# High and low part of a product's weights interleaved element by element

## What is computed

```python
x = fwht(x * SU_ug) / SCALE                       # 4096 tokens of 512
x_up = x @ W_up.T * (Wscale_ug[:INTER] * SCALE)    # INTER = 2048
x_gate = x @ W_gate.T * (Wscale_ug[INTER:] * SCALE)
x = silu(x_gate) * x_up
x = fwht(x * SU_dp) / SCALE
x = x @ W_down.T * (Wscale_dp * SCALE)
```

## Time and profile before

| | |
|---|---|
| median of 3 runs | 1592.2 us (1590.52 to 1594.0) |
| the profiled execution, its own time | 1590.71 us |
| its span, first to last instruction | 1588.9 us |
| granted TensorE clock, mean | 0.993 |
| PE busy | 1537.9 us (97%) |
| weight loads (PEld) busy | 1385.6 us (87%) |
| DVE busy | 1040.3 us (65%) |
| ACT busy | 616.2 us (39%) |
| POOL busy | 465.6 us (29%) |

### The profile page before, as it was taken

How to read it: one execution, slowest core, us unless ns; L and a number is a source line. 1 busy time by engine, 2 the same in 40 slices (tenths; PEclk the granted TensorE clock), 3 DMA queues, 4 the chain that set the end, 5 groups by cost and what they waited for, 6 DMA issues and landing times.

```text
span 1588.9 us, 26579 instructions
## 1 busy us (share of the span) xinstructions
PE 1537.9 (97%) x10280; PEld 1385.6 (87%) x10280; DVE 1040.3 (65%) x1771; ACT 616.2 (39%) x1257; POOL 465.6 (29%) x584
## 2 busy tenths in 40 slices
PE   6999999999998799999999999999999999999997
PEld 5987988888887688889999999999999999999996
DVE  6766776677676699875575475566466557557544
ACT  4153244235225555433433343343343333333322
POOL 5365456447337533500030030030040021013001
PEclk9999999999999999999999999999999999999999
DMA  7031122122222497587668677857776867766861
GB/s 270 1 120 60 34 87 93 34 81 100 70 77 84 185 374 275 212 293 278 236 218 297 220 253 246 279 204 257 268 245 220 307 203 258 276 242 212 281 229 63
DMA packets 92060, 307.44 MB, mean 193 GB/s; under 512 B 9888, under 2 KB 10272, under 8 KB 90144
## 3 DMA queue, kind: packets, MB, share of 16 engines
q1 hardware_dynamic: 90928, 301.54, 53.8%
q10 hardware_dynamic: 1008, 4.20, 0.7%
HBM read 255.37 MB, written 50.33 MB: 192 GB/s over the span
## 4 chain that ended last, share of the span: by engine, by line
PE 61%; DVE 5%; ACT 1%; DMA 1%; issue 1%; SPq 0%; POOL 0%; ACTq 0%; POOLq 0%; DVEq 0%
PE ff_bank_b L1840 16%; PE ff_bank_c L1840 10%; PE ff_bank_a L1840 10%; PE ff_acc L105 7%; PE ff_acc L107 7%; PE ff_acc L106 7%; DVE ff_d_lo L1639 2%; DMA gu_scratch<-ff_ring 1%; DVE ff_ring L1629 1%; PE ff_x_ps L1791 1%; ACT at_union L578 1%; PE ff_x_ps L1811 1%; PE ff_x_ps L1799 0%; DVE ff_c L1685 0%; PE ff_x_ps L1800 0%
## 5 line engine op out<-in xcount | busy, mean ns | idle before, releaser
L1840 PE MATMUL ff_bank_b<-ff_x_hi,ff_ring 128*128 128x256 f32 x1536 | 303.5, 280 | 4.5 <-DVE ff_c L1685 4.2
L1840 PEld LDWEIGHTS ff_bank_b<-ff_x_hi,ff_ring 128*128 128x128 f32 x1536 | 248.6, 188 | 6.3 <-issue 4.5
L1840 PE MATMUL ff_bank_b<-ff_x_lo,ff_ring 128*128 128x256 f32 x768 | 214.7, 280 | 0.0
L105 PE MATMUL ff_acc<-ff_d_hi,ff_h_hi 128*128 128x512 f32 x512 | 203.9, 398 | 2.7 <-DVE ff_d_lo L1639 2.7
L1840 PE MATMUL ff_bank_c<-ff_x_hi,ff_ring 128*128 128x256 f32 x1024 | 205.8, 284 | 0.0
L1840 PE MATMUL ff_bank_a<-ff_x_hi,ff_ring 128*128 128x256 f32 x1024 | 203.5, 282 | 0.0
L107 PE MATMUL ff_acc<-ff_d_hi,ff_h_lo 128*128 128x512 f32 x512 | 199.8, 390 | 0.0
L106 PE MATMUL ff_acc<-ff_d_lo,ff_h_hi 128*128 128x512 f32 x512 | 199.4, 389 | 0.0
L1840 PEld LDWEIGHTS ff_bank_c<-ff_x_hi,ff_ring 128*128 128x128 f32 x1024 | 166.2, 189 | 2.2 <-issue 2.0
L1840 PEld LDWEIGHTS ff_bank_a<-ff_x_hi,ff_ring 128*128 128x128 f32 x1024 | 165.3, 188 | 2.7 <-DVE ff_ring L1629 0.2
L1679 DVE TENSOR_TENSOR ff_c<-ff_bank_b,ff_c 128x512 f32<-128x512 f32 x64 | 44.2, 690 | 163.8 <-PE ff_bank_b L1840 163.8
(11 more groups left out here) (306 smaller groups left out, 3523.7 us busy)
## 6 DMA issues: line engine op xcount, KB each, us to landing
ff_ring<-gu_scratch SPq DMA_DIRECT2D x392, 512.0 KB, 4.9
gu_scratch<-ff_ring SPq DMA_DIRECT2D x56, 512.0 KB, 7.6
at_xt<-in_xt SPq DMA_DIRECT2D x4, 2048.0 KB, 8.4
at_xn<-in_x SPq DMA_DIRECT2D x32, 256.0 KB, 3.0
x_scratch<-at_x SPq DMA_DIRECT2D x32, 256.0 KB, 2.0
ff_raw<-in_wgu SPq DMA_DIRECT2D x8, 1024.0 KB, 7.7
at_wd_a<-in_wd SPq DMA_DIRECT2D x8, 512.0 KB, 4.1
mixed_scratch<-at_wd_a SPq DMA_DIRECT2D x8, 512.0 KB, 3.5
```

Source lines behind the costliest of these rows:

```text
L105: pe.matmul(out, lhs_hi, rhs_hi, start=first, stop=False)
L1840: i = pe.matmul(bank[:, m, :], r[:, a, m, c, :], b[:, k, c, :], start=(k < 3 and m == 0 and c == 0 and b is x_hi and a == 0), stop=(m == 1 ...
```

## The change

The tile's shape goes from [part, m, c, column] to [m, c, column, part]: the high and the low part of an element lie side by side, 4 bytes each. The scratch in DRAM has the same shape. So the ACT and the DVE instruction that make the tile write every second element (and DVE reads the high part in that step), and a weight load reads 128 elements with a step of 8 bytes between them, where they were packed at 4. The transfers move the same 4 KB of each partition in one piece. The token tiles of block 0 in slots 5 to 7 keep their place and are packed: the new function `half` gives for them the same views that `both` gave before.

```diff
-        ring = [sb(f"ring{i}", [P, 2, 2, 2, P], F32R) for i in range(RING)]
+        ring = [sb(f"ring{i}", [P, 2, 2, P, 2], F32R) for i in range(RING)]
@@
         def both(slot, part):
-            return ring[slot][:, part, :, :, :].rearrange("p m c n -> p (m c n)")
-
-
-        begin_hi = [xs_hi[:, :], both(5, 0), both(6, 0), both(7, 0)]
-        begin_lo = [xs_lo[:, :], both(5, 1), both(6, 1), both(7, 1)]
+            return ring[slot][:, :, :, :, part].rearrange("p m c n -> p (m c n)")
+
+        def half(slot, part):
+            return ring[slot][:, part, :, :, :].rearrange("p c n a -> p (c n a)")
+
+        begin_hi = [xs_hi[:, :], half(5, 0), half(6, 0), half(7, 0)]
+        begin_lo = [xs_lo[:, :], half(5, 1), half(6, 1), half(7, 1)]
@@
-                            i = pe.matmul(bank[:, m, :], r[:, a, m, c, :], b[:, k, c, :], start=(k < 3 and m == 0 and c == 0 and b is x_hi and a == 0),
+                            i = pe.matmul(bank[:, m, :], r[:, m, c, :, a], b[:, k, c, :], start=(k < 3 and m == 0 and c == 0 and b is x_hi and a == 0),
@@
-    gu_dram = nc.dram_tensor("gu_scratch", [PRODUCTS, P, 2, 2, 2, P], F32, kind="Internal").ap()
+    gu_dram = nc.dram_tensor("gu_scratch", [PRODUCTS, P, 2, 2, P, 2], F32, kind="Internal").ap()
```

## The result

The changed kernel takes 1605.3 us as the median of four runs (1603.3 to 1608.3), the kernel before 1592.1 in the same comparison: 1.0087 times as long, 95% interval 1.0074 to 1.0099. It is slower by some 13 us. The forecast was no change, with 0.26 for slower; the time lies inside the stated range, but the likeliest case did not come true.

The account below looks back on a forecast made before the run. PE's matmul pace, set by the moving stream, was taken to bound blocks 1 on, with DVE mattering in block 0. All terms summed to 0, +-2.7 us, on 1590.7 us, giving a median of 1592; the 8-in-10 range was 1586 to 1636.

Parts of the forecast that it names:

- the likeliest case: Whole kernel: no change in time, forecast median 1592 us, own range 1589 to 1596, chance 0.72.
- What bounds the kernel: From block 1 on, PE's matmul pace, 117.5 ns each, a load having 5.6 ns to spare; block 0 also DVE.
- The price of the step: Extra cost of reading or writing every second element: taken as zero for weight loads and tile writes.
- The longer of load and stream sets the pace: Products: a 111.9 ns load hides under a 117.5 ns matmul; only what exceeds 5.6 ns more is paid, 5376 times.
- The first rival: Weight loads: 32 further 16-byte pieces add 13.8 ns, pace 125.7 ns, 44 us more, 1635 us; chance 0.09.
- my second rival: Weight loads: every column takes its 0.83 ns twice, pace 218 ns, 540 us more, 2131 us; chance 0.08.
- The writes: ACT and DVE making the tiles with a step: zero added, against upper ends of 0.41 and 0.52 us an instruction.
- Transfers: 56 stores and 392 loads of 512 KB, still one 4 KB piece in each partition: zero cost.
- the token tiles: Block 0's tiles in slots 5 to 7, packed and read at the same addresses: zero cost.
- the place of the data: Loads touch 1 KB of a partition instead of 512 bytes: +-0.5 ns a load, 2.7 us in all.

Follow-up runs that it names:

- e3: Kernel before, each 256-column matmul of the products cut into two of 128, each with its own packed load of the same weights: 2167.9 us.
- e7: Kernel before, packed loads, the last 32 of 256 moving columns left out of every product in blocks 1 to 7: 1564.4 us.
- e4: Changed kernel, each 256-column matmul of the products cut into two of 128, each with its own stepped load of the same weights: 2230.5 us.
- e5: Changed kernel with the tile reordered to [c, column, m, part], so loads read with a step of 16 bytes, matmuls whole: 2196.8 us.
- e13: Kernel before, packed tiles, but the products' weight loads read with a step of 12 bytes, taking other elements than they should: 1882.3 us.
- e14: Kernel before, packed loads, but the products' moving operand reads 256 columns with a step of 8 bytes, other elements than it should: 2168.3 us.
- e8: Changed kernel, stepped loads, the last 32 of 256 moving columns left out of every product in blocks 1 to 7: 1596.3 us.
- e10: Kernel before, packed, with only 64 moving columns and 64 loaded weight columns in the products of blocks 1 to 7: 1438.0 us.
- e11: Changed kernel, stepped, with only 64 moving columns and 64 loaded weight columns in the products of blocks 1 to 7: 1448.0 us.
- e1: Changed kernel with high and low part in separate tile halves again, output halves interleaved so loads keep the 8-byte step: 1606.1 us, 1.0094 times the kernel before.
- e9: Changed kernel with only 64 of 256 moving columns in the products of blocks 1 to 7, all weight columns still loaded: 1964.3 us.
- e6: Changed kernel with a load step of 16 bytes and each product matmul cut into two of 128 moving columns: 3575.8 us.

## Why the prediction was wrong

**What bounds the kernel** held: from block 1 on nothing but PE's pace, block 0 with DVE beside it. The reading that a load has room for 5.6 ns held to half a nanosecond: e3 and e7 give 111.5 and 111.7 ns for a packed load where it sets the pace, I had 111.9.

**The price of the step** is the step that failed. For the weight loads I took zero, on the ground that the stepped load goes through 16 bytes in 1.66 ns and the stream through 16 bytes in 1.7. The runs show 6.6 ns a load in its place (e3 and e4: 111.5 and 118.1 ns), just more than the slack of about 6; the pace went from 117.5 to 120.0 and the time up by 13 us. The argument failed by its own figures: 1.66 is less than 1.7 (1.72 from the row), so the stepped load did ask for new pieces faster than anything in the trace was shown to get them. The load's own figure is 1.82 (e5, e13): 64 x 1.82 = 116.5 ns and some 1.6 over, 118.1 in e4. And the stream's rate was no proof of room above it: e14 shows its time going from 117.5 to 226.7 ns with twice the pieces at the same number of columns, so at full clock it already stood at the limit for pieces, or within a few per cent of it. The excess of a stepped column is small, 0.91 against 0.83 ns, but it was set against a slack of one twentieth.

The Trainium skill says in SBUF — State Buffer, section Door 1: The DMA port swizzle, that two hits on a 16-byte line absorb the access. The runs agree that the line is 16 bytes (e13) and that one hit in a line is dear (233 ns), and they differ on two hits: at 2.4 GHz two columns take 1.66 ns and their line 1.82, and the load is 6.6 ns longer; at 1.2 GHz two columns take 3.3 ns, and the step is free, as the page has it. For the packed load, the same skill's page TensorE: Matmul & The Clock Gate, section LDWEIGHTS (loading the stationary operand), has columns / 1.2 ns, 106.7; the 106 ns worked out from the recorded durations agree, at 2.4 GHz. One load after another takes 111.5 ns, and at 1.2 GHz 213.

**The longer of load and stream sets the pace** failed too, by 2 ns. By that rule 118.1 would have cost 0.6 ns x 5376 = 3 us, within 0.2%. Measured are 120.0 and 13 us. e8 shows that the rule holds with 224 columns and not at the near tie. So of the 2.5 ns, 0.6 are the load's excess over the stream and about 1.9 come from the tie, if 117.5 is the stream's own time; why a tie costs anything stays open.

**The first rival** had the right part of the kernel, a load that grows with its pieces, with 13.8 ns in place of 6.6 and 44 us in place of 13. But it charged pieces on top of the columns; e5, e13 and the half-clock rows of e10 and e11 show that the two run side by side and the slower counts. The doubled column, my second rival, was near the size for a step of 16 bytes (a pace of 218 ns forecast, 233 measured), and far off for the step of 8.

**The writes.** ACT's 50 ns follow the same figure, from 0.80 to about 0.9 ns an element; I had zero, on the ground that 16 bytes in 1.6 ns are no faster than the stream's 1.7, which they are. DVE at 1.02 ns an element is slower than a piece with two, and its zero held (686 to 692 ns). Block 0 as a whole took 149.9 us from its first product to block 1's, against 149.3, its slower loads included, so the writes cost next to nothing. **Transfers**, **the token tiles** and **the place of the data** show no cost, as forecast: the pace accounts for the loss, and e1, with another order in the tile, is not told apart from the changed kernel.

## What to carry to other kernels

Count the 16-byte pieces of an operand in each partition, not only its columns, for weight loads, streams and writes: in this kernel a piece took about 1.8 ns on each. What that means depends on how fast the reader or writer takes its columns. For weight loads and ACT's writes, at full clock, two fp32 in a piece cost 6 to 9%, for DVE's writes about 1%, and one in a piece makes ACT's and DVE's instructions 1.6 to 1.8 times as long and a load twice. A moving stream already takes its four columns in about the time of a piece, so for it two in a piece cost double. Where the trace shows an engine's rate, ask first what limits it before lending that rate to another. And a load that is nearly as long as the matmul that covers it is no longer free: here, at 118.1 against 117.5 ns, it cost 2 ns more than the longer of the two.

## What was not expected of the hardware

- At full clock a packed fp32r stream seems to be at the limit for pieces already: 256 columns in 64 pieces take 117.5 ns, 512 in 128 pieces 227.4, and 256 in 128 pieces 226.7. At half clock 512 packed columns take 427 ns, and 256 in 128 pieces still 230.
- A weight load takes two cycles of TensorE's clock for a column (0.83 ns at 2.4 GHz, 1.67 at 1.2), while the 1.82 ns for a piece are the same at both levels.
- The granted clock fell to 0.50 for stretches in e9 and e6, where a matmul streams 64 and 128 columns for a load of 118 and 233 ns, at a PE that the trace shows as busy without a gap. What sets it is not shown.
